# Graph attention on one core: the output projection of two heads at a time, with heads moved between partitions by DMA

## What is computed

```
h = max(layernorm(x), 0)
q, k, v = h @ Wq + bq, h @ Wk + bk, h @ Wv + bv          # 8 heads of 64
scores = leaky_relu(q k^T / 8 + edge_bias[adj], 0.2)     # where adj > 0, else -1e9
out = softmax(scores) v, heads side by side, @ Wp + bp
x = x + out
```

## Time and profile before

| | |
|---|---|
| median of 3 runs | 1039.76 us (1039.28 to 1040.35) |
| profiled execution | 1040.02 us, of which the span is 1037.7 us |
| busy in the span | PE 982.5 us (95%), DVE 913.8 (88%), ACT 777.2 (75%), POOL 486.8 (47%) |
| DMA | 125.20 MB in 190760 packets |
| TensorE clock granted, mean | 0.989 |

### The profile page before, as it was taken

One profiled execution on the slowest core, in us unless ns is written; L12 is line 12 of the kernel. 1 busy time (PEld: TensorE's weight loads), 2 busy tenths in 40 slices (PEclk: granted clock), 3 DMA queues, 4 the chain that ended last, 5 costly groups with the idle time before them and its releaser, 6 DMA issues.

```text
span 1037.7 us, 28703 instructions
## 1 busy us (share of the span) xinstructions
PE 982.5 (95%) x9056; PEld 969.0 (93%) x9056; DVE 913.8 (88%) x3409; ACT 777.2 (75%) x1737; POOL 486.8 (47%) x865
## 2 busy tenths in 40 slices
PE   4568999999999999999999999999999999999996
PEld 4458999999999999999999999999999999999995
DVE  3858999899998899989998899989998899989984
ACT  3576887887787877777877787778777887788762
POOL 1002454555454545454544555455445544555454
PEclk9997999999999999999999999999999999999998
DMA  7574344434353434434443443434343344434220
GB/s 173 162 230 118 116 128 120 136 95 141 104 142 99 129 123 118 131 110 133 124 122 105 121 124 113 138 108 126 121 134 111 109 129 119 137 100 116 82 68 9
DMA packets 190760, 125.20 MB, mean 121 GB/s; under 512 B 32832, under 2 KB 180300, under 8 KB 190604
## 3 DMA queue, kind: packets, MB, share of 16 engines
q1 hardware_dynamic: 189812, 122.75, 40.5%
q10 hardware_dynamic: 792, 0.53, 0.2%
HBM read 79.19 MB, written 44.04 MB: 119 GB/s over the span
## 4 chain that ended last, share of the span: by engine, by line
PE 83%; DVE 10%; issue 2%; DMA 1%; ACT 1%; POOL 1%; SPq 0%; ACTq 0%; POOLq 0%; DVEq 0%
PE bank L1222 19%; PE bank L1253 10%; PE bank L1175 10%; PE bank L1210 8%; PE bank L1312 6%; PE bank L1164 6%; PE bank L1165 5%; PE bank L1199 5%; PE bank L1187 5%; PE bank L1230 3%; DVE w L1658 2%; DVE w L1681 1%; PE bank L1238 1%; DVE o_all L1757 1%; DVE q_lo L1632 1%
## 5 line engine op out<-in xcount | busy, mean ns | idle before, releaser
L1034 POOL TENSOR_SCALAR a_line<-w,a_bias 128x256 f32<-128x256 f32 x512 | 263.1, 514 | 451.9 <-DVE w L1681 412.1
L1222 PE MATMUL bank<-pt,nat_sb 128*65 128x128 f32 x2048 | 265.4, 273 | 0.1
L1658 DVE CUSTOM_DVE_ANT_0 w<-bank,mask_rows 128x256 f32<-128x256 f32 x512 | 196.1, 419 | 67.6 <-issue 56.5
L1441 ACT ACTIVATE pt<-bank 128x512 f32<-128x512 f32 x256 | 154.0, 601 | 110.4 <-PE bank L1175 105.5
L1681 DVE SCALAR_TENSOR_TENSOR w<-w,shift,a_line 128x256 f32<-128x256 f32 x512 | 230.2, 489 | 2.5 <-POOL a_line L1034 2.5
L1222 PEld LDWEIGHTS bank<-pt,nat_sb 128*65 128x65 f32 x2048 | 230.7, 138 | 0.6 <-issue 0.6
L1670 DVE TENSOR_TENSOR onehot<-val,counts_to 128x512 fp32r<-128x512 f32 x256 | 181.5, 709 | 2.2
L1423 ACT ACTIVATE mask_own<-bank,mask_bias 128x512 bf16<-128x512 f32 x256 | 175.4, 685 | 1.2 <-PE bank L1199 1.2
L1175 PE MATMUL bank<-ident,w 128*128 128x128 f32 x1024 | 153.5, 272 | 0.0
L1432 ACT ACTIVATE t_sb<-bank 128x512 fp32r<-128x512 f32 x256 | 150.5, 588 | 3.3 <-PE bank L1187 3.2
L1164 PE MATMUL bank<-t_sb,q_hi 128*128 128x256 f32 x512 | 143.4, 302 | 0.1
(11 more groups left out here) (135 smaller groups left out, 1626.6 us busy)
## 6 DMA issues: line engine op xcount, KB each, us to landing
adj_in<-in_adj_dram SPq DMA_DIRECT2D x64, 512.0 KB, 3.8
mask_store<-mask_own SPq DMA_DIRECT2D x64, 512.0 KB, 3.6
mask_rows<-mask_store SPq DMA_DIRECT2D x512, 64.0 KB, 2.4
nl_store<-nl_ring SPq DMA_DIRECT2D x7, 512.0 KB, 4.2
stack_store<-stage SPq DMA_DIRECT2D x7, 512.0 KB, 3.1
h_stack<-stack_store SPq DMA_DIRECT2D x7, 512.0 KB, 4.6
h_nl<-nl_store SPq DMA_DIRECT2D x28, 128.0 KB, 3.8
x_res<-in_x_dram SPq DMA_DIRECT2D x16, 128.0 KB, 2.2
```

The source lines that it names most:

```text
L1034: nc.gpsimd.tensor_scalar(a_line[:, i % 2, :], w[:, i, :], 5.0, a_bias[:, i:i + 1], ALU.mult, ALU.add)\
L1222: last = pe.matmul(o_part[0:D + 1, P * u:P * u + P], nat_sb[:, t % 2, p % 4 * 2 + u, k, :], pt[:, p % 2, u, k, :], start=(k == 0), stop=(k ...
L1658: nc.vector.tensor_tensor_reduce(w[:, i, :], row_bank[:, SLOTS * u:SLOTS * u + SLOTS], mask_rows[:, t % 2, p % 4 * 2 + u, :], 0.25, LEAST_ ...
```

## The change

TensorE projects two heads at once. `w_pair` holds for each of the 4 pairs of heads a 128x128 matrix with the two folded 64x64 matrices on its diagonal blocks and zeros elsewhere. For that the weighed keys of an even and an odd head must stand on partitions 0 to 63 and 64 to 127: after ACT's copy (the buffer is now called `o_turned`) SP issues three DMAs per tile (`move_o`, lag 26, mod 2, right behind `move_masks`), two of 64x4x128 values (128 KB each) and one of 8x128 (4 KB), which puts the sums of the 8 heads on 8 rows. `project` waits for all three. It has 2 matmuls of 128x128 by 128 columns per call, and the first call has one more, of 8x128 by 8 columns, which turns the sums. `norm`'s lower bound and reciprocal now run once per tile on 8 columns; the `summed` wait of its first call moves behind them.

The lags change: `COUNT` stays at 6 (mod 2) and `TURN_A` goes from 5 to 7 (mod 3), `project` goes from 27 and 28 to 28 and 29 (mod 0 and 1), `norm` from 28 and 29 to 29 and 30, the sum over heads from 30 to 31, the output store from 31 to 32 (mod 0).

```diff
-    LOAD, CONV, TURN_A, COUNT, USED, RANK, VAL, ONEHOT = 0, 4, 5, 6, 7, 8, 9, 9
+    LOAD, CONV, COUNT, TURN_A, USED, RANK, VAL, ONEHOT = 0, 4, 6, 7, 7, 8, 9, 9
-    SCORE, A_LINE, Y, TURN, PV, X_ADD, PROJ, NORM, SUM, OUT = 17, 19, 20, 21, 22, 24, 27, 28, 30, 31
+    SCORE, A_LINE, Y, TURN, PV, X_ADD, MOVE_O, PROJ, NORM, SUM, OUT = 17, 19, 20, 21, 22, 24, 26, 28, 29, 31, 32
...
+            def move_o(b, t):
+                n, par = TPG * b + t, t % 2
+                sp.wait_ge(o_copied, 4 * n + 4)
+                if later(n, 2):
+                    sp.wait_ge(proj_done, 2 * n - 2)
+                heads = o_turned[0:D, par].rearrange("p (c a) q -> p c a q", a=2)
+                for a, rows in enumerate((slice(0, D), slice(D, P))):
+                    sp.dma_start(o_pairs[rows, par], heads[:, :, a]).then_inc(o_moved[par], 16)
+                sp.dma_start(den_rows[0:H, par], o_turned[D:D + 1, par]).then_inc(o_moved[par], 16)
...
                 t = tile(b, s, MASK_OUT)
                 if t is not None:
                     move_masks(b, t)
+                t = tile(b, s, MOVE_O)
+                if t is not None:
+                    move_o(b, t)
...
             def project(b, t, e, s):
                 n = TPG * b + t
-                pe.wait_ge(o_copied, 4 * n + 4)
-                free(adj_bank_uses, b, s, len(list(adj_bank_uses(b, s))) - 1)
-                for h in range(4):
-                    last = pe.matmul(adj_bank[:, (D + 1) * h:(D + 1) * h + D + 1], ot_sb[0:D + 1, t % 2, 4 * e + h, :],
-                                     w_ext[0:D + 1, 4 * e + h, :], start=True, stop=True)
+                pe.wait_ge(o_moved[t % 2], 48 * (n // 2) + 48)
+                free(adj_bank_uses, b, s, 0)
+                for c in range(2):
+                    last = pe.matmul(adj_bank[:, P * c:P * c + P], o_pairs[:, t % 2, 2 * e + c, :], w_pair[:, 2 * e + c, :],
+                                     start=True, stop=True)
+                if e == 0:
+                    last = pe.matmul(adj_bank[:, 2 * P:2 * P + H], den_rows[0:H, t % 2, :], ident[0:H, 0:H],
+                                     start=True, stop=True)
                 last.then_inc(proj_done, 1)
...
             def convert(b, t):
                 if later(n, 2):
                     pool.wait_ge(cnt_done, n - 1)
+                    pool.wait_ge(a_turned, n - 1)
...
-                    pe.matmul(misc[:, 0:D], mean_rep[:, :], w_sum[:, :], start=True, stop=True).then_inc(vec_done, 1)
+                    for a in range(2):
+                        last = pe.matmul(misc[:, 0:D], mean_rep[:, :], w_sum[:, a, :], start=(a == 0), stop=(a == 1))
+                    last.then_inc(vec_done, 1)
```

More of the change, by code:

```diff
@@ L258, in preln_graph_attention @@
         o_copied = sem("o_copied")
+        o_moved = [sem(f"o_moved{i}") for i in range(2)]
         proj_done = sem("proj_done")
@@ L666, in dense_scalar @@
                 for rows in (slice(0, D), slice(D, P)):
-                    nc.scalar.activation(vp_hi[rows, :].rearrange("p (h d) -> p h d", h=H), w_ext[0:D, :, 0:D],
-                                         ACT.Copy).then_inc(v_weights, 1)
+                    for a, heads in enumerate((slice(0, D), slice(D, P))):
+                        last = nc.scalar.activation(vp_hi[rows, :].rearrange("p (c a d) -> p a c d", a=2, d=D)[:, a],
+                                                    w_pair[heads, :, D * a:D * a + D], ACT.Copy)
+                    last.then_inc(v_weights, 1)
                 def q_hi_parts(b, k):
@@ L738, in dense_vector @@
                 for rows in (slice(0, D), slice(D, P)):
-                    nc.vector.tensor_tensor(vp_lo[rows, :].rearrange("p (h d) -> p h d", h=H), w_ext[0:D, :, 0:D],
-                                            vp_hi[rows, :].rearrange("p (h d) -> p h d", h=H).bitcast(F32), ALU.subtract)\
-                        .then_inc(v_weights, 1)
+                    for a, heads in enumerate((slice(0, D), slice(D, P))):
+                        lo, hi = (part[at, :].rearrange("p (c a d) -> p a c d", a=2, d=D)[:, a]
+                                  for part, at in ((vp_lo, rows), (vp_hi, heads)))
+                        last = nc.vector.tensor_tensor(lo, w_pair[heads, :, D * a:D * a + D], hi.bitcast(F32), ALU.subtract)
+                    last.then_inc(v_weights, 1)
                 def add_beta(g):
@@ L1115, in adj_bank_uses @@
             def adj_bank_uses(b, s):
+                t = tile(b, s, COUNT)
+                if t is not None:
+                    yield cnt_ready, TPG * b + t + 1
                 t = tile(b, s, TURN_A)
@@ L1118, in adj_bank_uses @@
                     yield adj_copied, TPG * b + t + 1
-                t = tile(b, s, COUNT)
-                if t is not None:
-                    yield cnt_ready, TPG * b + t + 1
                 due = piece(b, s, PROJ, 2)
@@ L1275, in step @@
                     natural(b, p)
+                t = tile(b, s, COUNT)
+                if t is not None:
+                    count(b, t, s)
                 t = tile(b, s, TURN_A)
@@ L1278, in step @@
                     turn_adj(b, t, s)
-                t = tile(b, s, COUNT)
-                if t is not None:
-                    count(b, t, s)
                 due = piece(b, s, PROJ, 2)
@@ L1738, in norm @@
                 dve.wait_ge(proj_done, 2 * n + e + 1)
-                if e == 0 and later(n):
-                    dve.wait_ge(summed, n)
-                parts = adj_bank[:, 0:4 * (D + 1)].rearrange("p (h d) -> p h d", d=D + 1)
-                nc.vector.tensor_scalar(den[:, heads], parts[:, :, D], 1e-30, None, ALU.max).then_inc(den_ready, 1)
+                parts = adj_bank[:, 0:2 * P].rearrange("p (h d) -> p h d", d=D)
                 if e == 0:
-                    nc.vector.tensor_scalar(alone[:, :], parts[:, 0, D:D + 1], 0.5, None, ALU.is_lt).then_inc(alone_ready, 1)
-                dve.wait_ge(den_ready, 2 * n + e + 1)
-                nc.vector.reciprocal(den_inv[:, heads], den[:, heads]).then_inc(den_inv_ready, 1)
-                if e == 0:
+                    sums = adj_bank[:, 2 * P:2 * P + H]
+                    nc.vector.tensor_scalar(den[:, :], sums, 1e-30, None, ALU.max).then_inc(den_ready, 1)
+                    nc.vector.tensor_scalar(alone[:, :], sums[:, 0:1], 0.5, None, ALU.is_lt).then_inc(alone_ready, 1)
+                    dve.wait_ge(den_ready, n + 1)
+                    nc.vector.reciprocal(den_inv[:, :], den[:, :]).then_inc(den_inv_ready, 1)
                     dve.wait_ge(alone_ready, n + 1)
@@ L1796, in _ @@
                 if s == 18:
-                    for rows in both:
-                        last = nc.vector.tensor_reduce(w_sum[rows, :], w_ext[0:D, :, 0:D].rearrange("p h d -> p d h"), AX_X, ALU.add)
+                    for a, heads in enumerate(both):
+                        for rows in both:
+                            last = nc.vector.tensor_reduce(w_sum[rows, a, :], w_pair[heads, :, D * a:D * a + D]
+                                                           .rearrange("p c d -> p d c"), AX_X, ALU.add)
                     last.then_inc(w_sum_ready, 1)
```

31 lines of the change are left out of this document (16 added, 15 removed).

## The result

The changed kernel takes **1162.77 us** (median of 4 runs, 1161.35 to 1169.65), the kernel before beside it 1039.84: a ratio of 1.1195, 95% interval 1.1151 to 1.124. It is 12% slower, 123 us, where 18 were forecast. The profiled execution took 1162.23 us, its span is 1160.4, the mean granted clock 0.937 instead of 0.989.

What follows compares the result with a forecast made beforehand. PE, busy 95% of the span, was taken as the bound; a new loop through the copies would make tiles 15.07 us instead of 14.81. Sum: 1040.02 + 17 for the loop + 1 for the ends = 1058 us, range 1020 to 1086.

Steps and rivals of the forecast that it cites:

- Part 3, up to the moves: SP after the mask store: first read issued at 3.88 us, all eight reads issued by 7.77 us.
- Part 3, the copies, 3.05: From the end of SP's eight reads, three copies are issued and landed in 3.05 us, 2.0 of it the last landing.
- rival of copies that land early: Copies within SBUF land sooner, 2.45 us instead of 3.05, giving 1027 us; 22 in 100.
- Part 3, from projection to store, 4.25: From PE's first projection of a tile to the next mask store: 4.25 us, 0.23 less through the shorter projection.
- Sum of Part 3: Loop of store, reads, copies, projection and next store: 7.77 + 3.05 + 4.25 = 15.07 us per tile instead of 14.81.
- Part 1, PE's work, 0.69 less: PE's two projection calls per tile cost 0.69 and 0.46 us, 1.15 instead of 1.84, at 0.115 per record.
- Part 2, the places, 0.99 less together with Part 1: Moved steps and shorter projections cut PE's own work and gaps by 0.99 us per tile, if DVE keeps up.
- The first thing late is the second `project`, waiting for L1757: If the cover at the new places were gone, PE's second projection would wait for DVE's first `norm`, 420 ns.
- Part 4, the ends, +1: Ramp unchanged; in the drain the copies add about 3 us, partly overlapped, so +1 us.
- Worse queueing: Rival: copies behind the reads take 3.8 us for 3.05, or projections 0.17 a record; 1100 us, 12 in 100.
- Not waited for: Rival: PE never waits for the copies and gains its whole 0.99 us per tile; 982 us, 8 in 100.
- Edits at nothing: Edits priced at zero: `copy_o`'s and POOL's waits, small matmuls and ramp reductions, later `adj` load, 16.8 MB more traffic.

Runs made afterwards that it cites:

- e3_warm: Changed kernel with seven f32 128x128 matmuls into unused columns put before PE's wait for the copies, so PE works instead of idling: 1138.82 us.
- e1_no_wait: Changed kernel with all three copies issued, but the projection does not wait for them and reads a fixed buffer of ones: 1039.17 us.
- f2_sums_later: e2_moves_first with DVE's subtraction from the adjacency's square sums, which waits for ACT's copy, moved two steps later: 1031.9 us.
- e2_moves_first: Changed kernel with the three copies issued between the mask store and the wait for its landing, instead of behind the eight reads: 1043.16 us.
- f1_old_lags: Paired projection with copies issued right behind the mask store, and all lags, order and bank waits of the kernel before: 1032.01 us.
- h3_old_lags_late_x: f1_old_lags with DVE's addition to `x_res` moved from the first `norm` to behind the second's product: 1027.75 us.
- h2: Control: the kernel before with only DVE's addition to `x_res` moved from the first `norm` to behind the second's product: 1034.33 us.
- f4_conv_later: f2_sums_later with POOL's conversion of `adj` one step later (lag 5): 1038.39 us.
- f3_lags_sums: Kernel before (65-column projection, no copies) with the new lags, order and bank waits, and DVE's square-sums subtraction two steps later: 1078.59 us.

## Why the prediction was wrong

The forecast was 1058, in the range 1020 to 1086; the time is 1163. The direction, the wait (PE's first projection of each tile, released by a DMA into `den_rows`), and the loop that it closes were right. Step by step:

- **Part 3, up to the moves: right.** First read 3.41 us after the store for 3.88, the eight reads issued at 7.57 for 7.77. 0.20 us better than forecast.
- **Part 3, the copies, 3.05: too small by 0.64.** The landing was nearly right: from the start of the `den_rows` issue to the projection are 2.14 us in the mean, 1.96 at least, for 2.0. The issues were not. The prediction priced three at "the 0.43 to 0.45 of the neighbours" and 0.1 for the odd long one. They take these times (min, median, max in ns):

```profile
L926 SPq DMA_DIRECT2D o_pairs<-o_turned x128: 608/622/1658, 116.5 to 1146.7; - x128
L927 SPq DMA_DIRECT2D den_rows<-o_turned x64: 704/709/762, 117.9 to 1147.4; - x64
```

The third starts 1.55 us after the end of the reads, not 1.05, and the projection comes 3.69 after it. The rival of copies that land early is refuted: the source in SBUF buys nothing against the reads' 2.0 to 2.4 of the earlier trace rows. DMA: Bandwidth & Descriptors of the Trainium skill (Latency and other measured facts) puts most of the fixed 2 us on the receipt from the target memory, with HBM as the slowest; the trace does not bear that out here, as the copies touch no HBM and take 2.0 to 2.1.
- **Part 3, from projection to store, 4.25: 5.45 in the run.** The largest error, 1.20 us per tile, 72 us. 0.85 of it is TensorE's clock, shown by e3_warm (4.60). The prediction took a wait of 1.25 us as its own length. But in 29 of the 60 tiles PE runs at half its clock behind the stall, on the loop, which makes the next store later. TensorE: Matmul & The Clock Gate of the Trainium skill (Part 1) says that the engine is slowed after idling; the traces agree that it happens, with 3.4 us at 0.50 behind 1.87 idle. The rule given there speaks of longer gaps than most of these; here the measurement decides, and it shows the half clock behind 1.04 and full clock behind 2.24. The prediction, which had the earlier trace rows at 1.00, did not ask what its own wait would do to them. The other 0.35 is there at full clock too (4.48 before, 4.25 forecast, 4.60 in e3_warm): 0.23 of it is the shorter first call, which takes 0.94 and so saves nothing, and 0.12 was not followed up.
- Sum of Part 3: -0.20 + 0.64 + 1.20 = 1.64; 15.07 + 1.64 = 16.71, the measured tile.
- **Part 1, PE's work, 0.69 less: 0.43 at best.** Before, the two calls take 0.92 and 0.89 in the mean; the prediction read both as 0.92. Its 0.115 per record holds for the second call (0.44 for 0.46), and 0.17, its upper bound, did not come. The first call costs 0.94 for 0.69, since the small matmul adds 0.48, not 0.23. The rule of TensorE: Matmul & The Clock Gate of the Trainium skill (LDWEIGHTS) that the prediction set beside the row gave 0.64, and misses the small matmul in the same way. With the old lags only about 0.21 per tile shows (14.81 - 14.60).
- **Part 2, the places, 0.99 less together with Part 1: the sign is wrong.** "The bank's other waits cost nothing as long as DVE keeps up": it doesn't. Beside the 65-column projection the places cost 48.6 us: 9 from `square_sums_adj`, whose wait for `adj_copied` the prediction overlooked, 28 from POOL's conversion stopping DVE, about 11 left open. In the paired kernel they cost 11.2, all gone with the subtraction moved. The prediction looked at how much work each step holds on PE and DVE, and not at what runs beside what. "The first thing late is the second `project`, waiting for L1757" was right as a place, and is what e1_no_wait shows. In the changed kernel PE hardly waits for DVE's `norm` (1.3 us); the DMA wait covers it, and may cover the 18.2 us of `square_sums_adj` too. With the DMA wait gone the 0.99 per tile shrinks to 0.16 (14.81 - 14.64, f2_sums_later): PE works 0.41 less per tile (849.65 of 872 us at 14.64 for 864.38 at 14.81) and is idle 0.38 for 0.13, nearly all of it in waits for DVE's `norm` (21.8 us in the window). This, and the 11 us of the subtraction, is why e2_moves_first takes 1043 and not 982.
- **Part 4, the ends, +1: +8.** The last tiles pay each copy with nothing to hide it. Here the last two sums over the heads end 7.1 us apart, each behind a wait for DVE, which waits for the projection, which waits for the copies.

```profile
1146.93 1.65 POOL L1042 TENSOR_TENSOR o_all<-o_all 128x256 f32<-128x256 f32 x3 [3.88 <-DVE o_all L1782]
1148.66 0.32 POOL L1045 TENSOR_TENSOR x_res<-x_res,o_all 128x64 f32<-128x64 f32 x1
1154.03 1.65 POOL L1042 TENSOR_TENSOR o_all<-o_all 128x256 f32<-128x256 f32 x3 [5.05 <-DVE o_all L1782]
```

- **The rivals.** "Worse queueing" (1100) had the right side for a wrong reason: its 3.8 for the copies is near the measured 3.69, but by the issues and not by the landing, so that was luck. "Not waited for" did not come true; with its condition made in e1_no_wait the time is 1039 and not 982.
- **Edits at nothing:** the later `adj` load, `copy_o`'s wait, the traffic: with e2_moves_first they and all else come to 3.9 us above the kernel before, though there they stand against the smaller work of PE, so this is no bound on each.

What the idea is worth, set right: paired projection, copies issued in SP's idle time, old places (f1_old_lags), 7.4 us below the kernel before beside it; with the later addition (h3_old_lags_late_x) 12.7, of which 4.3 (against f1_old_lags) to 6.1 (h2) are the addition's.

## What to carry to other kernels

Price a new wait by its length and by the clock after it: if the stalled engine stands on the loop that ends the wait, a slow stretch makes the next round longer, here in about half of the rounds. Before reckoning a DMA's landing, ask where its issue stands on the queue; here moving three issues in front of a wait that SP had anyway was worth 120 us. When steps change places, look at what each operation now runs beside: a tiny DVE operation with two SBUF inputs that meets a long one on POOL costs the rest of that one, and the profile shows it as a higher mean duration, not as a wait. Moving the long one away only helps if it meets nothing else of that kind, as f4_conv_later shows. And a price found beside one version of the work (48.6 us for the places) need not hold beside another (11.2).

## What was not expected of the hardware

- SP needs 0.62 us to issue a copy within SBUF of 64x4x128 values and 0.71 us for one of a single row onto 8 rows, against 0.43 for a 512 KB load; the landing, about 2.1 us, is as long as that of reads from HBM.
- Behind an idle 1.87 us PE ran 3.4 us at a granted clock of 0.50; behind 0.70 it kept 1.00, and behind 2.24 in another tile too. In 29 of 60 tiles the clock fell, behind stalls of 1.04 us and more.
- A 0.15 us DVE operation took 0.99 us in each of 25 meetings with a POOL operation of 1.43 us, and ended with it (f3_lags_sums).
- An f32 matmul of 8x8, two records, took 0.31 us by the distance of starts, and 0.48 was what it added to its call, as much as two of 128x128 by 128 columns.
